# Three experts on one slot as column tiles of 64, 32 and 32 rows, 69 slots in place of 72

## The reference

```python
logits = flat @ router_w.T                       # 2048 x 32 experts
topk_w, topk_ids = top_k(softmax(logits), 4)     # 4 experts for each row
topk_w = topk_w / topk_w.sum(-1)
xs = rows of flat, sorted by expert              # 8192 rows, 256 for an expert in the mean
gu = ragged_dot(xs, w1, group_sizes)             # w1[e]: 512 x 512
act = silu(gu[:, :256]) * gu[:, 256:]
ys = ragged_dot(act, w2, group_sizes)            # w2[e]: 256 x 512
routed = sum over the 4 experts of topk_w * ys
shared = (silu(flat @ sg) * (flat @ su)) @ sd
out = residual + routed + shared
```

## Time and profile before

| | us |
|---|---|
| median of 3 executions | 1701.81 (1701.61 to 1704.36) |
| the profiled execution, its own time | 1702.38 |
| its span, first to last instruction | 1700.6 |
| mean granted TensorE clock, share of 2.4 GHz | 0.968 |

### The profile page before, as it was taken

The page is one execution under the profiler, slowest core; times in us unless marked ns, Lnnn a source line. Parts: engine busy times, 40 slices in busy tenths (PEclk is TensorE's granted clock), DMA queues, the critical chain, the costliest instruction groups (busy, mean ns, idle before and its releaser), DMA issues. The chain is left out here.

```text
span 1700.6 us, 14562 instructions
## 1 busy us (share of the span) xinstructions
PE 1529.2 (90%) x4334; PEld 690.0 (41%) x4335; DVE 1160.3 (68%) x1502; ACT 734.6 (43%) x1215; POOL 1063.2 (63%) x533
## 2 busy tenths in 40 slices
PE   5668998889988899988887788999999999999997
PEld 2323433334433344333333334544444444444443
DVE  3498999999999998999999973456213333333332
ACT  4476666676566765756675635111111111111110
POOL 0099898999879998999998971000004454444543
PEclk9889999999999999999999999999999999999999
DMA  3530113411124201115100042014117778877783
GB/s 118 218 139 8 41 45 102 164 45 35 33 65 173 87 26 39 28 37 199 33 28 8 19 149 87 32 31 167 51 39 199 193 186 230 239 199 200 185 236 54
DMA packets 63693, 177.11 MB, mean 104 GB/s; under 512 B 10240, under 2 KB 15104, under 8 KB 54912
## 3 DMA queue, kind: packets, MB, share of 16 engines
q1 hardware_dynamic: 47360, 137.24, 23.0%
q0 software_dynamic: 16256, 38.94, 11.6%
HBM read 143.56 MB, written 32.56 MB: 104 GB/s over the span
## 5 line engine op out<-in xcount | busy, mean ns | idle before, releaser
L1257 POOL TENSOR_TENSOR h<-h,c_rep 128x2048 f32<-128x2048 f32 x128 | 579.6, 4532 | 29.5 <-DVE h L909 24.5
L1446 PE MATMUL bank<-h,ident 128*128 128x512 f32 x916 | 450.0, 635 | 94.9 <-POOL h L1257 73.0
L673 ACT ACTIVATE bank<-delta,a_neg 128x512 f32<-128x512 f32 x512 | 335.9, 682 | 179.5 <-DVE h L909 178.7
L1446 PEld LDWEIGHTS bank<-h,ident 128*128 128x128 f32 x916 | 181.2, 203 | 339.5 <-issue 212.3
L909 DVE TENSOR_TENSOR_SCAN h<-bank,state,h 128x512 f32<-128x512 f32 x256 | 305.9, 1259 | 0.5 <-ACT bank L673 0.5
L909 DVE TENSOR_TENSOR_SCAN h<-bank,h 128x512 f32<-128x512 f32 x256 | 290.7, 1200 | 2.1 <-ACT bank L673 1.9
L899 DVE TENSOR_TENSOR h<-bank,b_rep 128x2048 f32<-128x2048 f32 (+1 forms) x105 | 227.4, 2185 | 42.3 <-ACT bank L666 31.4
L1752 PE MATMUL h_ps<-w_ring,xT 128*128 128x512 f32 x512 | 241.3, 594 | 1.7 <-PEq L374 1.7
L1667 DVE TENSOR_TENSOR xT<-xT_ps,norm_w_f 128x512 f32<-128x512 f32 x70 | 48.4, 692 | 238.8 <-PE xT_ps L1732 232.1
L1572 POOL DMA_INDIRECT out<-y,slot_token x64 | 101.1, 1579 | 136.7 <-DMA out<-y,slot_token 63.3
L1645 ACT ACTIVATE aT<-aT_ps 128x256 f32<-128x256 f32 x72 | 27.7, 384 | 268.9 <-PE aT_ps L1761 265.0
(11 more groups left out here) (234 smaller groups left out, 1669.2 us busy)
## 6 DMA issues: line engine op xcount, KB each, us to landing
w_ring<-in_w SPq DMA_DIRECT2D x32, 1024.0 KB, 5.0
b_rep<-bcd SPq DMA_DIRECT2D x16, 1024.0 KB, 6.9
c_rep<-bcd SPq DMA_DIRECT2D x16, 1024.0 KB, 4.9
w_ring<-in_w SPq DMA_DIRECT2D x32, 512.0 KB, 6.1
w_in<-in_w_in_x SPq DMA_DIRECT2D x32, 256.0 KB, 2.7
w_res<-in_w_in_res SPq DMA_DIRECT2D x32, 256.0 KB, 2.6
xa<-in_x SPq DMA_DIRECT2D x20, 256.0 KB, 3.0
xb<-in_x SPq DMA_DIRECT2D x16, 256.0 KB, 3.0
```

Source lines behind the costliest of these rows:

```text
L673: eng.activation(da[j][:], delta[:, g % 2], ACT.Exp, scale=a_neg[:, col:col + 1])\
L1257: ins = eng.tensor_tensor(h[:, q], h[:, q], c_rep[:, Q * q:Q * q + Q, :], ALU.mult)
L1446: ins = eng.matmul(y_ps[:], c.ident[:], h[:, q, j, :], start=False, stop=(q == NQ - 1 and j == Q - 1))
```

## The change

Experts are ranked by their row counts (a compare of all against all, ties by index), and two tables of straight lines in the rank give each its place and the number of its first row. The five largest get two slots and 64 rows of a mixed slot (room 320), the next ten two slots and 32 rows (288), the other seventeen two slots (256). A group has one of the seventeen, one of the five, and two of the ten; its mixed slot is shared by the latter three. Five such groups of nine slots are followed by twelve places of two slots each: 45 + 24 = 69 slots. `each` takes the place of `both` in the slots. In the five groups there are four batches in place of five, with three scatters for a mixed slot; there are eight y buffers in place of six, five blocks of spare rows in place of three, and a third copy of the slot list. `NT`, the width of the list, goes from 126 to 125.

```diff
-GROUPS, SPARE, PART = E // RING, E // 2, P // 2
-SLOTS = 2 * RING + 1
-MAIN = GROUPS * SLOTS
-REST = (T - 2 * P - PART) * TOPK // P
+GROUPS, PART, QUARTER = E // RING, P // 2, P // 4
+SHARED, SLOTS = 5, 2 * RING + 1
+MAIN = SHARED * SLOTS + (GROUPS - SHARED) * 2 * RING
+SPARE = 5
+REST = (T - 2 * P - PART) * TOPK // P + 2
...
-                for n in range(3):
+                for n in range(SPARE):
                     eng.dma_start(dram.flat[T + n * P:T + (n + 1) * P, :], blank[:]).then_inc(F["blank_stored"], 16)
                     eng.dma_start(dram.out[TT + n], blank[:, 0:DM]).then_inc(F["blank_stored"], 16)
-                eng.wait_ge(F["blank_stored"], 96)
+                eng.wait_ge(F["blank_stored"], 32 * SPARE)
...
+                eng.dma_start(c.slot_last[0:QUARTER, :], c.slot_token[P - QUARTER:P, :]).then_inc(F["upper_listed"], 16)
                 store_base(TT - 1)
-                eng.wait_ge(F["upper_listed"], 16)
+                eng.wait_ge(F["upper_listed"], 32)
...
+                    ch.add(eng.scalar_tensor_tensor(load_key[:], cnt[:], float(E), iota[:, 0:E], ALU.mult, ALU.subtract))
+                    ch.settle()
+                    ch.add(eng.tensor_tensor(above[:], load_key[:].unsqueeze(1).to_broadcast([P, E, E]), row(load_key[:], E), ALU.is_gt))
+                    ch.settle()
+                    ch.add(eng.tensor_reduce(order[:], above[:], AX.X, ALU.add))
...
+                def by_order(out, lines):
+
+                    plain, a, b, c_ = steps
+                    (a0, b0), (n1, a1, b1, o1), (n2, a2, b2, o2), (n3, a3, b3, o3) = lines
+                    ch.add(eng.tensor_scalar(plain[:], order[:], a0, b0, ALU.mult, ALU.add))
+                    for term, slope, level in ((a, a1, b1), (b, a2, b2), (c_, a3, b3)):
+                        ch.add(eng.tensor_scalar(term[:], order[:], slope, level, ALU.mult, ALU.add))
+                    ch.settle()
+                    for term, by_odd in ((a, o1), (b, o2), (c_, o3)):
+                        if by_odd:
+                            ch.add(eng.scalar_tensor_tensor(term[:], odd[:], by_odd, term[:], ALU.mult, ALU.add))
+                    ch.settle()
+                    for term, below in ((a, n1), (b, n2), (c_, n3)):
+                        ch.add(eng.scalar_tensor_tensor(term[:], order[:], float(below), term[:], ALU.is_lt, ALU.mult))
+                    ch.settle()
+                    ch.add(eng.tensor_tensor(plain[:], plain[:], a[:], ALU.add))
+                    ch.add(eng.tensor_tensor(b[:], b[:], c_[:], ALU.add))
+                    ch.settle()
+                    ch.add(eng.tensor_tensor(out[:], plain[:], b[:], ALU.add))
...
+                    wide, thirds, some = SHARED, 3 * SHARED, 4 * SHARED
+                    tile = float(P)
+                    by_order(place, ((1.0, 0.0), (some, 3.0, -60.0, 0.0), (thirds, -2.0, 51.0, 1.0), (wide, 2.0, 10.0, -1.0)))
+                    by_order(first_at, ((2 * tile, 5 * tile), (some, 7 * tile, -140 * tile, 0.0),
+                                        (thirds, -4.5 * tile, 115 * tile, 2.5 * tile), (wide, 4.5 * tile, 22 * tile, -2.5 * tile)))
+                    ch.add(eng.tensor_scalar(third_at[:], odd[:], 224.0, -544.0, ALU.mult, ALU.add))
+                    ch.add(eng.tensor_scalar(room[:], order[:], float(wide), float(QUARTER), ALU.is_lt, ALU.mult))
+                    ch.add(eng.tensor_scalar(beyond[:], order[:], float(thirds), float(QUARTER), ALU.is_lt, ALU.mult))
...
-        KEPT = 6
+        KEPT = 8
...
-        MIXED = RING
+        MIXED, JOINT = RING, SHARED * SLOTS
         halves = (slice(0, PART), slice(PART, P))
+        pieces = (slice(0, PART), slice(PART, PART + QUARTER), slice(PART + QUARTER, P))
 
         def mixed(n):
-            return n % SLOTS == MIXED
+            return n < JOINT and n % SLOTS == MIXED
 
         def places(n):
 
+            if n >= JOINT:
+                return [SHARED * RING + (n - JOINT) // 2]
             m, k = divmod(n, SLOTS)
             if k == MIXED:
-                return [m * RING, m * RING + 1]
+                return [m * RING + 1, m * RING + 2, m * RING + 3]
             return [m * RING + (k if k < MIXED else k - 1) // 2]
 
         def last_slot(place):
 
             m, v = divmod(place, RING)
-            return m * SLOTS + (MIXED if v < 2 else 2 * v + 2)
+            return m * SLOTS + (1, MIXED, 6, 8)[v] if m < SHARED else JOINT + 2 * (place - SHARED * RING) + 1
 
         def shares(n):
 
-            return n + 1 + (n + SLOTS - MIXED) // SLOTS
-
-        BATCHES = (2, 3, 1, 2, 2)
+            return n + 1 + 2 * min(SHARED, (n + SLOTS - MIXED) // SLOTS)
+
+        def batch_size(b):
+            return 3 if b < SHARED * RING and b % RING else 2
 
         def batch_of(n):
 
-            m, k = divmod(n, SLOTS)
-            return m * len(BATCHES) + (0, 0, 1, 1, 2, 3, 3, 4, 4)[k]
+            return places(n)[-1]
 
         def landed(eng, b):
 
             if b >= 0:
-                eng.wait_ge(added[b % 2], 16 * sum(BATCHES[a % len(BATCHES)] for a in range(b % 2, b + 1, 2)))
+                eng.wait_ge(added[b % 2], 16 * sum(batch_size(a) for a in range(b % 2, b + 1, 2)))
 
         def all_landed(eng):
-            for b in (GROUPS * len(BATCHES) - 2, GROUPS * len(BATCHES) - 1):
+            for b in (E - 2, E - 1):
...
+                for m in range(SHARED):
+                    first, b = m * SLOTS, m * RING
+                    for n in (first, first + 1):
+                        turn(n)
+                        scatter(n, b)
+                    for n in (first + 2, first + 3):
+                        turn(n)
+                        scatter(n, b + 1)
+                    turn(first + MIXED)
+                    scatter_piece(first + MIXED, 0, b + 1)
+                    scatter_piece(first + MIXED, 1, b + 2)
+                    for n in (first + 5, first + 6):
+                        turn(n)
+                        scatter(n, b + 2)
+                    scatter_piece(first + MIXED, 2, b + 3)
+                    for n in (first + 7, first + 8):
+                        turn(n)
+                        scatter(n, b + 3)
+                for n in range(JOINT, MAIN):
+                    turn(n)
+                    scatter(n, places(n)[0])
...
+                    rows = pieces if mixed(n) else (slice(0, P),)
                     for place, part in zip(places(n), rows):
...
+                def each(out, turned, ring, k, n_k):
+
+                    for v in range(3):
+                        ins = eng.matmul(out[pieces[v], :], turned[:, k, pieces[v]], ring[:, 1 + v, k, :],
+                                         start=(k == 0), stop=(k == n_k - 1))
+                    return ins
...
-                            ins = both(h_ps[i], xT[:, i], c.w1r, k, KC)
+                            ins = each(h_ps[i], xT[:, i], c.w1r, k, KC)
...
-                            ins = both(y_ps[i], aT[:, i], c.w2r, k, FC)
+                            ins = each(y_ps[i], aT[:, i], c.w2r, k, FC)
```

More of the change, by code:

```diff
@@ L190, in front @@
         cnt, zero = inside("cnt", [P, E]), inside("zero", [P, E])
[L191 to L194, removed]
+        load_key, order, odd = inside("load_key", [P, E]), inside("order", [P, E]), inside("odd", [P, E])
+        order_i, place = inside("order_i", [P, E], I32), inside("place", [P, E])
+        steps = [inside(f"step{n}", [P, E]) for n in range(4)]
         first_at, third_at = inside("first_at", [P, E]), inside("third_at", [P, E])
@@ L200, in front @@
         posn, hit = inside("posn", [P, TT, E]), inside("hit", [P, TT, E])
-        cmp = over("cmp", "posn", [P, E, NM])
+        cmp, above = over("cmp", "posn", [P, E, NM]), over("above", "posn", [P, E, E])
         lo_i, hi_i = inside("lo_i", [P, TT * TOPK], I32), inside("hi_i", [P, TT * TOPK], I32)
@@ L1048, in route_counts @@
-                    ch.add(eng.tensor_scalar(left[:], full_rank[:, E - 1:E], -1.0, float(SPARE), ALU.mult, ALU.add))
+                    ch.add(eng.tensor_scalar(order_i[:], order_i[:], 1, None, ALU.bitwise_and))
                     ch.settle()
-                    ch.add(eng.tensor_scalar(moved[:], plain[:], float(SPARE), left[:, 0:1], ALU.is_ge, ALU.mult))
-                    ch.add(eng.scalar_tensor_tensor(wide[:], plain[:], float(SPARE), full[:], ALU.is_ge, ALU.max))
+                    ch.add(eng.tensor_copy(odd[:], order_i[:]))
@@ L1068, in route_homes @@
+                    ch.add(eng.scalar_tensor_tensor(room[:], room[:], 2 * tile, beyond[:], ALU.add, ALU.add))
+                    ch.settle()
                     ch.add(eng.tensor_tensor(beyond[:], cnt[:], room[:], ALU.subtract))
                     ch.settle()
-                    ch.add(eng.tensor_copy(odd[:], order_i[:]))
                     ch.add(eng.tensor_tensor(cmp[:], row(beyond[:], NM), thr[:].unsqueeze(1).to_broadcast([P, E, NM]), ALU.is_gt))
@@ L1587, in _, with turn @@
                 eng.wait_ge(c.base_stored, 16 * TT)
```

(28 more changed lines are left out.)

44 lines of the change are left out of this document (14 added, 30 removed).

## The result

The changed kernel takes 1711.64 us (median of 6, 1711.44 to 1716.39) where the kernel before takes 1702.12 in the same comparison: ratio 1.0056, 95% interval [1.0043, 1.0068]. Its profiled execution took 1711.74 us, with a span of 1710.0 and a mean granted clock of 0.967.

A forecast was written before the change was run, and what follows sets the result against it. TensorE, busy 425.52 of the expert stage's 427.30 us, was taken to bound the kernel. Terms of -20.3 and +32.0 gave +11.7 us, forecast 1713.5 us; own range 1706 to 1720, widened to 1680.5 to 1720 for the faster case.

The forecast's parts named there:

- What goes: Expert stage: three mixed slots fall away at 6.76 us each, 20.3 us less.
- What comes: TensorE, five remaining mixed slots: 15 stretches of four blocks, 4.00 us in place of 1.87, +32.0 us.
- The step that carried the row of a 128 to 64 change over to 64 and 32 columns: Mixed stretches: nothing of a new width enters while the old is in flight, taken to hold here too; block 1.00 us.
- The forecast's 0.09 gap and 0.05 for the open load: Each block: 0.09 us gap to the next width; first pass 0.48 instead of 0.43 as its weight load lies open.
- Rival 1: Mixed stretches: widths overlap where columns differ, so only the three dropped slots count; 1681.5 us, chance 0.24.
- Rival 2: Mixed stretches: widths exclude each other but the switch is free; +4.7 us, 1706.5 us, chance 0.10.
- Rival 3: Expert stage: rival 1 with a wait uncovered, the fourth expert's weights late or y held back; 1687 us, chance 0.04.
- the fourth expert's weights: Mixed slot: issued 17.2 us before they are needed, against a median landing of 6.1 us; cost 0.
- Rival 4: Mixed stretches: all three tiles run in a row, 32-tiles losing their overlap too; 1736 us, chance 0.04.
- Routing: Before the expert stage: steps up to in_rest take at most 8.4 us, 1.5 us of slack or more before TensorE asks.
- The oh_hi rows of 125: Routing, VectorE: 125 columns instead of 126, cost taken as 0; at most 5 us in all at double length.
- The four more blank stores: Start: four more 0.26 MB stores before w_out; even 10 us more stay hidden, first weights being used 26 us later.

The follow-up runs named there:

- e1: The changed kernel with its 64-row piece issued as two 32-wide tiles of the same weights: 1685.76 us, ratio to before 0.9887.
- e1b: The kernel of e1 run again with no edit, in another comparison: 1683.54 us, ratio to before 0.9890.
- e3: The kernel before (72 slots), only the lower half of each shared slot issued as two 32-wide tiles beside the 64-wide upper one: 1751.32 us, ratio 1.0289.
- e2: The changed kernel with each mixed stretch sorted by width, the 64-wide tile for both k, then the 32-wide ones: 1709.17 us, ratio to before 1.0039.
- e4: The kernel before (72 slots) with both halves of each shared slot issued as two 32-wide tiles each: 1701.78 us, ratio 0.9993.
- e6: The changed kernel with tile order 64, 32, 32 for even k and 32, 32, 64 for odd k, three blocks: 1712.63 us, ratio to before 1.0054.
- e5: The kernel of e1 with six y buffers in place of eight: 1682.15 us, ratio to before 0.9874.

## Why the prediction was right

**What bounds it.** The stage is TensorE's before and after: 2.2 us of waits, at its first and its last stretch. Every edit of a stretch came out in the stage to 0.1 us or so.

**What goes.** Three mixed slots at 6.76, 20.3 us: e1's 20.47 is this term, and some 0.2 us for stretches of 1.86 in place of 1.87.

**What comes.** Forecast 4 blocks of 1.00, 4.00 a stretch, measured 3.97; a slot of 13.15, measured 13.07; +32.0, measured 15 x (3.97 - 1.87) = +31.5. The sum of +11.7 stands against 11.27 in the stage. The span grew by 9.4 only; the other 1.9 us lie outside the stage, at its start and its end, where e1 and e1b differ by 3.73 and 1.08 us with no edit at all. That the median came within 1.9 us of the forecast is therefore part luck; the stage is what bears it out. The step that carried the row of a 128 to 64 change over to 64 and 32 columns held, e3 shows it by itself. What that step could not know, whether tiles on separate columns exclude each other too, the trace of after settles for this layout, and e2's two blocks in a row.

The runs divide the price into the two parts that the forecast had joined. All stretches fit one sum: 0.43 us for each pass of a block of one width, and 0.13 to 0.14 for each block. That is 4 x 0.43 + 0.14 = 1.86 (e1, e4; before 1.87), 8 x 0.43 + 2 x 0.13 = 3.70 (e2), + 3 x 0.137 = 3.85 (e6), + 4 x 0.1325 = 3.97 (changed, e3). Of the 2.10 us more, 1.72 are passes that no longer run beside each other, 0.4 are switches. The forecast's 0.09 gap and 0.05 for the open load are the 0.14.

The Trainium skill, "TensorEngine Tiling (Array Packing)", Key Properties, has the engine drained when the tiling mode changes. The trace agrees, in that nothing of the next width, not even a load, starts until the block in front has had its two passes of 0.43 us or more; 64 and 32 columns over the same 128 rows behave as two modes (e3). Its sentence that tiles operate independently held here only between tiles of one width: two 32-wide tiles in 0.98 us, but a 64-wide one beside them not at all.

**Rivals.** Rival 1 (overlap) is refuted: no 32-wide load stands inside a 64 block. Its time of 1681.5 is what the placement is worth where the widths agree (e1 and e1b: 1680.5 to 1686.9). Rival 2 (exclude, free switch) gave 3.54 a stretch, 3.44 and 0.10 at its end; the changed kernel takes 3.97 and e2, with half the switches, still 3.70. Rival 3 had two waits: y reaches DVE with six buffers but not TensorE (e5); the fourth expert's weights were issued at 1384.39 and used from 1401.58, the forecast's 17.2 us, and PE has no wait on them. Rival 4 (all in a row) is refuted by the 32 blocks of 0.98 us.

**Covers, from the trace of after.** Routing: DVE's steps up to in_rest take from 1122.16 to 1130.35 us, 8.2 (at most 8.4 was forecast), and TensorE asks at 1132.19, 1.8 us of slack. The oh_hi rows of 125 take 0.31. The four more blank stores put w_out at 93.96 instead of 91.19, and the weights behind it are used at 117.53 instead of 117.66. The rows of DVE, of PE and of SP:

```profile
1130.20 0.15 DVE L1105 TENSOR_SCALAR in_rest<-in_rest 128x1 f32<-128x1 f32 x1
...
1159.72 0.31 DVE L1153 TENSOR_SCALAR oh_hi<-iota_h,hi,tok 128x125 f16<-128x125 f16 x1
```

```profile
1132.19 0.22 PE L1437 MATMUL bank<-ident,at_place 128*1 128x32 f32 x2
...
117.53 1.02 PE L1392 MATMUL bank<-dtr,w_dt_sb 128*128 128x512 f32 x2
```

```profile
93.96 0.33 SPq L478 DMA_DIRECT2D w_out<-in_w_out  x1
...
1384.39 0.33 SPq L1558 DMA_DIRECT2D w_ring<-in_w  x1
```

POOL's scatters in pieces wait longer, 49.9 us for landings (8 times) and 34.7 for y (6), where before's waited 45.2 (7 times) and 25.9 (8). In the stage no engine waits for POOL itself, and DVE waits for landings twice, 0.9 us in all, even with eight y buffers; TensorE does not:

```profile
POOL out L1597 <- DMA out<-y,slot_token: 49.9, 8, 8.3
...
POOL out L1597 <- DVE y L1708: 34.7, 6, 8.8
```

**What was too wide.** The chance of 0.24 for rival 1 pulled the range down to 1680.5. Between 64 and 32 columns no row of before could exclude it, so some of that was due; the row of held-back loads spoke against it more than I gave it. The forecast's own range, 1706 to 1720, holds the result as well.

## What to carry to other kernels

In every run here column tiles ran beside each other only with tiles of the same width, although the 64-wide tile had columns 0 to 63 and the 32-wide ones 64 to 127. (All were fp32 over 128 rows with 512 moving columns; other types, shapes and widths were not run.) So cut a shared matmul into tiles of the smallest width in it (here two 32-wide tiles for the 64 rows: 31.7 us of stage between the changed kernel and e1, with more instructions). Sorting by width gets back only the switches. Before a slot is shared more finely, price the shared slot against the slots it removes: eight at 6.76 against five at 13.07 was a loss, five at 6.72 (e1's groups last 53.20) a gain of 1.1%.

## What the runs showed of the hardware that I had not expected

- Four 32-wide fp32 tiles of 512 moving columns take no longer than two 64-wide ones: 1.86 us for 16 records, 1.87 for 8. I had no row for it when I wrote the prediction; e1 and e4 expected it.
- The same code in front took a different time from one profiled execution to the next: the stage began between 1260.95 and 1263.06 us in the three profiles with the routing of before and between 1261.46 and 1267.73 in the six with the new one, while the stage itself agreed to 0.01 us between e1, e1b and e5. Here a change of 2 us is read from the stage's rows, not from a median of four. Between e1 and e1b it went with the granted clock; what sets that stays open.
